# Pointwise product on four tiles of TensorE, with two stored forms of the pixels and a ring of four pairs

## The reference

```python
h = einsum('bhwi,ic->bhwc', x, fc0_w) + fc0_b          # 64 channels, then to b c h w
for l in range(4):
    xf = rfft2(h)                                       # 16 x 16 modes at two corners are kept
    top = einsum('bixy,ioxy->boxy', xf[:, :, :16, :16], w1); bot = ...   # mixing of channels, mode by mode
    sc = irfft2(of)                                     # inverse transform
    y = sc + einsum('bihw,oi->bohw', h, pw_w[l]) + pw_b[l]    # the pointwise product
    h = gelu(batchnorm(y) * gamma[l] + beta[l])         # mean and variance over b, h, w
```

## Time and profile before

| | |
|---|---|
| median of 3 runs | 3084.08 us (3083.77 to 3089.99) |
| the profiled execution's own time | 3082.53 us |
| its span, first to last instruction | 3080.4 us |
| TensorE, VectorE, ScalarE busy | 2629.7, 1577.3, 1567.5 us |
| mean granted TensorE clock | 0.926 |
| stretch taken as layer 1's inverse stage (its first load starts at 782.03) | 782 to 1056 us |
| moved by DMA | 603.67 MB |

### The profile page before, as it was taken

How to read it: one execution, slowest core, us unless ns; L and a number is a source line. 1 busy time by engine, 2 the same in 40 slices (tenths; PEclk the granted TensorE clock), 3 DMA queues, 4 the chain that set the end, 5 groups by cost and what they waited for, 6 DMA issues and landing times. The chain is left out here.

```text
span 3080.4 us, 65084 instructions
## 1 busy us (share of the span) xinstructions
PE 2629.7 (85%) x27131; PEld 1694.6 (55%) x27131; DVE 1577.3 (51%) x2552; ACT 1567.5 (51%) x2659; POOL 191.7 (6%) x237
## 2 busy tenths in 40 slices
PE   7559998978899899669998977899799577882999
PEld 4556665648566566566665657566422156642444
DVE  3136666752466677326666752466500376746443
ACT  1213336742456677225566753355499567851333
POOL 0000000000000000000000000000000222220443
PEclk9779999988899999889999998899899888995999
DMA  7845448966899799669988967799665200001432
GB/s 241 246 127 172 168 164 311 322 192 172 252 294 291 273 328 308 140 187 288 295 283 299 322 203 179 233 291 296 221 225 178 51 1 1 1 1 40 94 88 63
DMA packets 243649, 603.67 MB, mean 196 GB/s; under 512 B 28415, under 2 KB 108991, under 8 KB 241087
## 3 DMA queue, kind: packets, MB, share of 16 engines
q1 hardware_dynamic: 243359, 599.51, 62.7%
HBM read 396.12 MB, written 203.93 MB: 195 GB/s over the span
## 5 line engine op out<-in xcount | busy, mean ns | idle before, releaser
L604 ACT ACTIVATE work<-P,small 128x512 f32<-128x512 f32 x512 | 323.8, 683 | 536.0 <-PE P L477 499.3
L371 PE MATMUL P<-cst,work 128*128 128x128 f32 (+1 forms) x3760 | 547.3, 285 | 48.9 <-ACT work L626 13.7
L371 PEld LDWEIGHTS P<-cst,work 128*128 128x128 f32 (+1 forms) x3760 | 410.4, 143 | 206.6 <-issue 157.6
L426 PE MATMUL P<-W,work 128*64 128x64 f32 x4096 | 283.6, 307 | 129.9 <-ACT work L575 129.5
L472 PE MATMUL P<-work,wbd 128*128 128x512 f32 x768 | 371.5, 606 | 0.0
L477 PEld LDWEIGHTS P<-cst,ATs 64*128 64x128 f32 x4096 | 248.4, 187 | 194.1 <-issue 194.1
L426 PEld LDWEIGHTS P<-W,work 128*64 128x64 f32 x4096 | 282.0, 239 | 132.4 <-issue 98.7
L738 DVE COPY ATs<-P 128x512 f32<-128x512 f32 x256 | 177.0, 692 | 327.5 <-PE P L371 327.5
L750 DVE BATCH_NORM_STATS2 W<-work 128x6 f32<-128x512 f32 x512 | 327.1, 680 | 19.8 <-ACT work L604 19.2
L477 PE MATMUL P<-cst,ATs 64*128 64x128 f32 x4096 | 297.5, 285 | 0.0
L780 DVE COPY work<-P 128x512 f32<-128x512 f32 x384 | 247.1, 684 | 73.0 <-PE P L371 72.9
(11 more groups left out here) (166 smaller groups left out, 3031.2 us busy)
## 6 DMA issues: line engine op xcount, KB each, us to landing
work<-z_d SPq DMA_DIRECT2D x384, 512.0 KB, 6.0
z_d<-work SPq DMA_DIRECT2D x256, 512.0 KB, 4.0
W<-in_wmix SPq DMA_DIRECT2D x96, 512.0 KB, 6.8
X_d<-work SPq DMA_DIRECT2D x128, 256.0 KB, 5.0
work<-X_d SPq DMA_DIRECT2D x32, 1024.0 KB, 12.4
G_d<-work SPq DMA_DIRECT2D x128, 256.0 KB, 3.3
work<-G_d SPq DMA_DIRECT2D x256, 128.0 KB, 5.4
hz<-z_d SPq DMA_DIRECT2D x64, 512.0 KB, 4.6
```

The source lines that it names most:

```text
L371: return nc.tensor.matmul(out, in_, ident[0:n, 0:n], start=True, stop=True, is_transpose=True)
L426: last = nc.tensor.matmul(P[n % 8][f * 64:f * 64 + 64, i * 64:i * 64 + 64], xm[:, :, x * 4 + y], W[:, 4 * (c + f) + y, x * 64:x * 64 + 64] ...
L604: nc.scalar.activation(y[:, h], P[4 + 2 * (a.q % 2) + h][:, :].rearrange("p (j n) -> p j n", n=128), ACT.Identity, bias=bias0 if first els ...
```

## The change

The pointwise product no longer uses one 128 by 128 weight matrix with two copies on its diagonal. It uses four products of 64 by 64, one for each pair of row half and column half of the array. An input row half x goes to output row half w, for the pixel half w of the columns. So the output has another form than the input: where the partitions' halves were the two images, they become the two halves of the pixels, and the reverse in the next layer (`image_half`). After four layers the form is the first again. To add up in the same banks, the spectral product L460 picks its image and its column half by this form and is cut in 32 products of 64 columns instead of 16 of 128. The constants i1, VectorE's copy to Ai, and in layers 1 and 3 the forward stage's source of F1 and ScalarE's two copies follow the form.

A step's outputs are now two pieces of 512 in two halves of ybuf; ybuf has twice the room (two buffers of 2048) and is stored after every second step, with two DMAs of 512 KB (`z_y`). ScalarE waits for a buffer's stores only at even q, and for the statistics four outputs later than before. Pixels are loaded in the order of quarters 0, 2, 1, 3 (`QCOL`). In layers 1 to 3 zbuf has four pairs, two of them in the part of W that isn't in use there, and the loads run eight steps further ahead. In all layers the mixed spectrum is loaded one pair earlier. In layer 0 the input's rows are loaded with two DMAs of 3 rows, and its weights wc6 are 128 by 128.

```diff
-    i1 = np.kron(np.eye(2), np.block([[c.T, s.T], [-s.T, c.T]]))
+    i1 = np.block([[c.T, s.T], [-s.T, c.T]]).reshape(2 * KY, 2, 2, SIDE // 2).transpose(0, 2, 1, 3).reshape(2 * KY, 128)
+    i1 = np.kron(np.eye(2), i1)
...
-        zbuf = [part(0, 4096), part(4096, 4096)]
+        zbuf = [part(0, 4096), part(4096, 4096)] + [W[:, i:i + 4, :].rearrange("p w n -> p (w n)") for i in (4, 8)]
...
-        ybuf = [part(16384, 1024), part(17408, 1024)]
+        ybuf = [part(12288, 2048), part(16384, 2048)]
...
+        z_y = z_d.rearrange("(t u) p (x k n) -> t u x k p n", u=2, x=2, k=2)
+
+        def image_half(l, x, w):
+
+            return (x, w) if l % 2 == 0 else (w, x)
+        QCOL = (0, 2, 1, 3)
...
+        def zslot(l, pair):
+
+            return pair % 4 if l else pair % 2
...
+        def ychunk(a, h):
+
+            o = h * 1024 + a.q % 2 * 512
+            return ybuf[a.q // 2][:, o:o + 512]
...
+                load_mixed(At(0, 0, 0, 0))
+
                 def step(t, u, q):
                     a = At(t, u, q, 0)
-                    if q == 0 and a.ok:
-                        wait(sp, "pI1", l * 32 + a.pair * 2 - 2)
-                        for v in range(2):
-                            for h in range(2):
-                                sp.dma_start(Gt[u][v * 64:v * 64 + 64, h * 512:h * 512 + 512], G_s[h, a.t, u, v]).then_inc(gl[u], 16)
+                    n = At(t, u, q, -4)
+                    if q == 0 and n.ok:
+                        wait(sp, "pI1", l * 32 + n.pair * 2 - 2)
+                        load_mixed(n)
                     b = At(t, u, q, 8)
-                    if b.ok:
+                    if b.ok and b.q % 2 == 1:
 
                         sp.wait_ge(S["eY"], l * 128 + b.s * 2 + 2)
-                        sp.dma_start(z_q[b.t, b.par, :, b.q], ybuf[b.q % 2]).then_inc(yst[b.q % 2], 16)
+                        for x in range(2):
+                            sp.dma_start(z_y[b.t, b.par, x, b.q // 2], ybuf[b.q // 2][:, x * 1024:x * 1024 + 1024]).then_inc(yst[b.q // 2], 16)
+                    load_pixels(a if first else At(t, u, q, -8))
+
+                def load_pixels(a):
                     if not a.ok:
                         return
-                    wait(sp, "pY", l * 128 + a.s * 2 - 14)
-                    o = slice(q * 1024, q * 1024 + 1024)
+                    if a.pair >= (2 if first else 4):
+                        sp.wait_ge(S["pY"], l * 128 + (a.pair - (2 if first else 4)) * 8 + a.q // 2 * 4 + 4)
+                    o, z, landed = slice(QCOL[a.q] * 1024, QCOL[a.q] * 1024 + 1024), zbuf[zslot(l, a.pair)], zl[zslot(l, a.pair)][a.q // 2]
                     if first:
-                        sp.dma_start(zbuf[u][0:6, o], x6_q[a.t, u, :, q]).then_inc(zl[u][q], 16)
+                        for h in range(2):
+                            sp.dma_start(z[h * 64:h * 64 + 3, o], x6_q[a.t, a.par, h, :, QCOL[a.q]]).then_inc(landed, 16)
                     else:
-                        sp.dma_start(zbuf[u][:, o], z_q[a.t, u, :, q]).then_inc(zl[u][q], 16)
+                        sp.dma_start(z[:, o], z_q[a.t, a.par, :, QCOL[a.q]]).then_inc(landed, 16)
+                if not first:
+                    for s in range(8):
+                        load_pixels(At(0, s // 4, s % 4, 0))
...
-                        for i in range(4):
-                            m = 2 * a.q + i
-                            for h in range(2):
+                        for m in range(8):
+                            for w in range(2):
+                                image, half = image_half(l, a.q // 2, w)
                                 for v in range(2):
-                                    o, x = slice(v * 64, v * 64 + 64), h * 512 + m * 64
-                                    last = nc.tensor.matmul(P[v][h * 64:h * 64 + 64, i * 128:i * 128 + 128], Gt[a.par][o, x:x + 64], i1c[o, v * 128:v * 128 + 128], start=True, stop=True)
+                                    o, x, k = slice(v * 64, v * 64 + 64), image * 512 + m * 64, v * 128 + half * 64
+                                    last = nc.tensor.matmul(P[v][w * 64:w * 64 + 64, m * 64:m * 64 + 64], Gt[a.par][o, x:x + 64], i1c[o, k:k + 64], start=True, stop=True)
                         last.then_inc(S["pI1"], 1)
...
-                            pe.wait_ge(S["z_gelu_c"], (l - 1) * 64 + a.s + 1)
+                            pe.wait_ge(S["z_gelu_c"], (l - 1) * 64 + a.pair * 4 + a.q // 2 * 2 + 2)
                         wait(pe, "eY", l * 128 + a.s * 2 - 2)
                         banks = P[4 + 2 * (a.q % 2):6 + 2 * (a.q % 2)]
-                        z = zbuf[a.par][0:rows, a.q * 1024:a.q * 1024 + 1024].rearrange("p (j s n) -> p s j n", s=2, n=128)
-                        for s in range(2):
-                            nc.tensor.matmul(banks[s][:, :].rearrange("p (j n) -> p j n", n=128), pw[0:rows, :], z[:, s], start=True, stop=False)
+                        for w in range(2):
+                            for x in range(2):
+                                o, n = slice(x * 64, x * 64 + 64), w * 2048 + a.q * 512
+                                nc.tensor.matmul(banks[x][w * 64:w * 64 + 64, :], pw[o, o], zbuf[zslot(l, a.pair)][o, n:n + 512], start=True, stop=False)
...
-                                src = hTq[a.s % 2][rows, :].rearrange("p (i c) -> p i c", c=128)[:, :, g * 32:g * 32 + 32]
+                                if l % 2 == 0:
+                                    src = hTq[a.s % 2][rows, :].rearrange("p (i c) -> p i c", c=128)[:, :, g * 32:g * 32 + 32]
...
+                                else:
+                                    src = hTq[a.s % 2][rows, :].rearrange("p (i h c) -> p i h c", h=2, c=64)[:, :, :, g * 16:g * 16 + 16]
...
-                        y = ybuf[a.q % 2].rearrange("p (j s n) -> p s j n", s=2, n=128)
                         for h in range(2):
                             act.wait_ge(S["pY"], l * 128 + a.s * 2 + h + 1)
-                            if h == 0:
-
-                                wait(act, yst[a.q % 2], stores_waited(l, a))
-                                wait(act, "eS", l * 128 + a.s * 2 - 2)
-                            nc.scalar.activation(y[:, h], P[4 + 2 * (a.q % 2) + h][:, :].rearrange("p (j n) -> p j n", n=128), ACT.Identity, bias=bias0 if first else pwb_c).then_inc(S["eY"], 1)
+                            if h == 0 and a.pair >= 1:
+
+                                if a.q % 2 == 0:
+                                    act.wait_ge(yst[a.q // 2], (l * 16 + a.pair) * 32)
+                                act.wait_ge(S["eS"], l * 128 + a.s * 2 - 6)
+                            nc.scalar.activation(ychunk(a, h), P[4 + 2 * (a.q % 2) + h][:, :], ACT.Identity, bias=bias0 if first else pwb_c).then_inc(S["eY"], 1)
...
-                        nc.vector.tensor_copy(Ai[a.par].rearrange("p (y k) -> p y k", k=2 * KX)[:, :, v * KX + 8 * b:v * KX + 8 * b + 8],
-                                              P[v][:, :].rearrange("p (k y) -> p y k", y=SIDE)).then_inc(S["eI1"], 1)
+                        nc.vector.tensor_copy(Ai[a.par].rearrange("p (y h z k) -> p h y z k", h=2, z=2, k=2 * KX)[:, b, :, :, v * KX:v * KX + KX],
+                                              P[v][:, :].rearrange("p (k y z) -> p y z k", k=KX, z=2)).then_inc(S["eI1"], 1)
```

More of the change, by code:

```diff
@@ L138, in build_fno @@
             "x0_load")}
-        zl = [[sem(f"zl{u}{q}") for q in range(4)] for u in range(2)]
+        zl = [[sem(f"zl{u}{q}") for q in range(2)] for u in range(4)]
         fz = [sem(f"fz{u}") for u in range(FR)]
@@ L197, in __init__, with zl_count @@
                 self.ok = not isinstance(self.pair, int) or 0 <= self.pair < PAIRS
+        def zslot(l, pair):
+            return pair % 4 if l else pair % 2
+        def zl_count(l, pair):
+            if l == 0:
+                return pair // 2 * 64 + 64
+            return (512 if pair % 4 < 2 else 0) + (l - 1) * 128 + pair // 4 * 32 + 32
+        def ychunk(a, h):
+            o = h * 1024 + a.q % 2 * 512
+            return ybuf[a.q // 2][:, o:o + 512]
         def over_steps(eng, body, last=PAIRS // 2 + 1):
@@ L301, in step @@
                     if first:
-                        sp.dma_start(zbuf[u][0:6, o], x6_q[a.t, u, :, q]).then_inc(zl[u][q], 16)
-                    else:
-                        sp.dma_start(zbuf[u][:, o], z_q[a.t, u, :, q]).then_inc(zl[u][q], 16)
+                        for h in range(2):
+                            sp.dma_start(z[h * 64:h * 64 + 3, o], x6_q[a.t, a.par, h, :, QCOL[a.q]]).then_inc(landed, 16)
+                    else:
+                        sp.dma_start(z[:, o], z_q[a.t, a.par, :, QCOL[a.q]]).then_inc(landed, 16)
@@ L433, in inv @@
                 if first:
-                    nc.tensor.matmul(P[7][0:6, 0:128], fc0Tbd, wbd[:, :], start=True, stop=True)
+                    nc.tensor.matmul(P[7][:, 0:128], fcp[:, :], wbd[:, :], start=True, stop=True)
```

(17 more changed lines are left out.)

35 lines of the change are left out of this document (20 added, 15 removed).

## The result

The changed kernel takes 2943.4 us (2939.4 to 2947.2), the kernel before 3085.2 us: a ratio of 0.954, interval 0.952 to 0.955.

The account below looks back on a forecast made before the run. TensorE was taken to set the pace of all four inverse stages, with transfers 7% from their limit in three. Layer 0 -24 and layers 1 to 3 -16 each gave -72: 3010.5, as a median 3012 us, range 2970 to 3055.

Parts of the forecast that it names:

- The pointwise product: Inverse stages: four quarters run together, so a step's product falls from 1.93 to 1.06 us, 55.7 us a layer.
- The direction: Whole kernel: faster than before, chance 0.87; same 0.03, slower 0.10.
- Spectral product: L460, inverse stages: weight loading sets each wave, so twice the records cost +0.88 us a half pair, 25.5 us a layer.
- the second rival: L460 does not double: half pair 6.3 us, layer 0 gains 55, other layers 19 each, total 2972; chance 0.12.
- two rows of other lines: L426 (57 ns a record) and L1314 (50 ns), read as showing that L460's waves don't shrink with their moving columns.
- The start: Inverse stages' start: three L460 groups at half clock, +1.75 us each: 5.3 us in layer 0, 3.9 in layers 1 to 3.
- The sentence that leaned on the Trainium skill: L460: by the rule of starts about 25 ns apart alone, sixteen waves cost +0.73 us instead of +0.88.
- Transfers in layers 1 to 3: Inverse stages: a pair needs 14.9 us of transfer, TensorE wants one every 14.4; +9 us a layer comes back.
- G_d of pair 1 is now issued behind eight pixel loads ... nothing: Start of inverse stages: at 407 GB/s G_d lands at about 797, when the later chain just needs it; no cost.
- The rival of late stores: Layers 1 to 3: paired stores land after the 8.6 us window; at 10.5 us +182 on -72, 3194; chance 0.09.

Follow-up runs that it names:

- run 7: Changed kernel with only half of each pixel load in layers 1 to 3 (512 of 1024 columns; outputs differ): 2876.4 us, ratio 0.933.
- run 1: Kernel before with only the spectral product L460 cut into products of 64 columns (64 records for 32, same results): 3091.3 us, ratio 1.002.
- run 4: Kernel before with mixing product L426 taking its 64 weight columns from neighbouring words instead of every 64th (outputs differ): 3048.0 us, ratio 0.988.
- run 9: Changed kernel with the pixel ring of layers 1 to 3 at two pairs and four output buffers: 2887.1 us, ratio 0.938.
- Run 5: Changed kernel with pair 1's G_d issued directly behind pair 0's, ahead of the pixel loads, in each inverse stage: 2944.8 us, ratio 0.955.
- run 6: Changed kernel with four output buffers of 2048 in place of two: 2917.2 us, ratio 0.945.
- runs 5 and 8: Changed kernel with pair 1's G_d issued ahead of the pixel loads: 2944.8 us; the same plus four output buffers: 2904.9 us, ratio 0.942.

## Why the prediction was wrong

**Right.** TensorE set the pace of all four inverse stages before. The pointwise product costs 1.04 to 1.09 us in quarters (1.06 forecast). VectorE and ScalarE hide their work: at 6.33 us a half pair TensorE has no gap in layer 0, nor in layer 1 of run 7, where ScalarE has its GELUs too. The forward stages did not grow. The direction was forecast with 0.87.

**The step that failed: "Spectral product", "I take +0.88".** It measured +0.06 (1.16 against 1.10) in each of 128 half pairs; run 1 shows it alone, as 2 to 4 us in the body of each stage. The term was 25.5 + 5.3 us in layer 0. With it gone, layer 0 gains 24 + 31 = 55, which is the second rival's sum, and 54 came. The prediction had the right rival with a chance of 0.12 and wrote for it "nothing but that L426's weights are strided". That was the point: run 4 shows the stride as the price. Its bound took two rows of other lines for the price of L460's own loads. The start had the same error. At the half clock 64 records of 64 columns take 1.98 us, as 32 of 128 did.

The sentence that leaned on the Trainium skill ("TensorE: Matmul & The Clock Gate", "Wait — 56ns, not 53.3ns?") fell with it. The floor of 25 ns from start to start that the Trainium skill states there would give 64 records 1.6 us. From L502's first start to L515's there is 0.98 us, 15 ns a record with four tiles in turn. The sum did not use that sentence.

**The step that was mis-sized: "Transfers in layers 1 to 3", "14.9 us of all sixteen engines" a pair.** A busy share of 0.93 at 294 GB/s was read as a limit near 316 GB/s, or 322 with the 1.02 that the prediction allowed. The changed kernel moved 339, and run 9 moved 362 at a share of 1.00: 13.0 us a pair. A share of 0.93 was not 93% of what the engines can do. So the bodies of layers 1 to 3 became 34 to 39 us shorter, and with the starts 28 to 30 us a layer were gained where 16 were forecast. This term is also why the second rival's total, 2972, missed: it had 19. That transfers limit layers 1 to 3 at all was right. At 6.33 us a half pair TensorE asks for 4.72 MB in 12.7 us, 373 GB/s, and 362 would stretch layer 0's body of 197 us to 203, an estimate from these two rates; run 9 has 201.4 to 206.0.

The 358 GB/s of the Trainium skill ("DMA: Bandwidth & Descriptors", Specifications) was the better guide here. Run 9 stands just above it, and in that run transfers are what is waited for.

**What was missed: the start.** "G_d of pair 1 is now issued behind eight pixel loads ... nothing" cost 8.9, 5.9 and 8.0 us in the three layers. It was said to land at about 797, 15 us after the first load's issue; in the changed kernel the third spectral product started 22.9 us after it (728.6 to 751.5). Two things were left out. The rate was taken as 407 GB/s, and in the stretch from 728.6 to 751.5 it was 299. And pair 2's four loads, issued behind G_d from 738.14 on, shared the engines with it: the trace has the first of them landed at 750.1 and the last of G_d's at 751.5. How much each cost was not tried apart. Run 5, with G_d ahead of all pixels, starts after 10.4 us, but its pair 2 then waits for the same reason.

**The rival of late stores** had the right mechanism and the wrong price. The window is 6.33 + 2.65 - 1.27 = 7.7 us and the stores landed 7.8 us after issue (median) where "about 6 to 7" were forecast, so ScalarE waited 30.5 us in 140. That ate part of the gain, 26 us of it by run 6, but did not turn it.

The measured parts add up: layer 0's body -54, those of layers 1 to 3 -163 together at layer 0's pace, +54 for what transfers cost them (16 to 20 each) and +23 for their starts, is -140, against 138.8 between the spans. Between the 72 forecast and the 140 measured lie two errors that made the forecast too small, a cost that is not there and a transfer limit set too low, and one that made it too large, the loss at the starts.

## What to carry to other kernels

Before a row from another line is used as a bound, compare what its instruction reads (stride, rows, tile) and the clock granted to it. One that differs in stride is no bound for a weight load, and an experiment that cuts the loop in the old kernel costs one run. A busy share of DMA near 1 is not a rate limit; look at the window that each buffer gives its transfer, reuse less write, against the landing time. And when a deeper ring is filled at a stage's start, follow every load that stands behind the fill, not the next one alone: moving one ahead moved the wait to the one after it (runs 5 and 8), and the ring of two, which has no such fill, was faster.

## What was not expected of the hardware

Four tiles of 64 by 64 hide their weight loads (135 ns each) behind 64 moving columns: 64 records in 0.98 us, start to start, which is 15 ns a record.

Weight loads with a stride of 64 words took 242 ns instead of 138, and in the mixing stages that is 37 us of this kernel.

The same traffic of a pair took 14.9 us of the sixteen engines at 294 GB/s and 13.0 at 362.
